# Attention and FFN kernel: high parts of the weights as copies on ScalarE; a small output, values and output weights placed in other steps

## What is computed

```python
def attn(x, W_K, W_Q, W_V, W_O):
    k = jnp.einsum('ihd,bpd->biph', W_K, x)
    q = jnp.einsum('ihd,bpd->biph', W_Q, x)
    v = jnp.einsum('ihd,bpd->biph', W_V, x)
    scores = jnp.einsum('biph,biqh->biqp', k, q)
    mask = jnp.tril(jnp.ones((pos, pos), dtype=x.dtype))
    masked = scores * mask - jnp.float32(10000000000.0) * (1.0 - mask)
    attn = jax.nn.softmax(masked / jnp.sqrt(jnp.float32(d_head)), axis=-1)
    z = jnp.einsum('biqp,biph->biqh', attn, v)
    z_flat = jnp.transpose(z, (0, 2, 1, 3)).reshape(b, pos, -1)
    return jnp.einsum('df,bqf->bqd', W_O, z_flat)

def ffn(x, W1, W2, W3):
    hidden = jax.nn.silu(x @ W1.T) * (x @ W3.T)
    return fwht(hidden) @ W2.T

xn = layernorm(x)
out = x + attn(xn, ...) + ffn(xn, ...)
```

## Time and profile before

| | us |
|---|---|
| three runs | 1448.01, 1448.76, 1451.03; median 1448.76 |
| the profiled execution | 1451.85, its span 1450.0 |
| PE busy | 1351.6 (93%) |
| GpSimd busy | 996.1 (69%) |
| VectorE, ScalarE busy | 957.7 (66%), 931.0 (64%) |

### The profile page before, as it was taken

The page is one execution under the profiler, slowest core; times in us unless marked ns, Lnnn a source line. Parts: engine busy times, 40 slices in busy tenths (PEclk is TensorE's granted clock), DMA queues, the critical chain, the costliest instruction groups (busy, mean ns, idle before and its releaser), DMA issues.

```text
span 1450.0 us, 26628 instructions
## 1 busy us (share of the span) xinstructions
PE 1351.6 (93%) x8104; PEld 1195.5 (82%) x8104; DVE 957.7 (66%) x2133; ACT 931.0 (64%) x1879; POOL 996.1 (69%) x660
## 2 busy tenths in 40 slices
PE   3989999969999999999999999999999999999985
PEld 2778888758888888888888888888888888888875
DVE  7743300277777777777777777777777767777760
ACT  3312244457777777777777777777777777777772
POOL 4420000066979797979797979797979787979785
PEclk8999999989999999999999999999999999999998
DMA  4100056579898989898988898888888888888884
GB/s 147 69 1 0 0 145 186 169 228 286 248 281 259 288 256 286 270 286 253 285 263 280 259 289 268 284 259 280 255 281 270 265 275 266 284 269 288 248 266 153
DMA packets 278459, 335.14 MB, mean 231 GB/s; under 512 B 62736, under 2 KB 251280, under 8 KB 273808
## 3 DMA queue, kind: packets, MB, share of 16 engines
q1 hardware_dynamic: 278416, 334.65, 73.6%
HBM read 173.08 MB, written 161.48 MB: 231 GB/s over the span
## 4 chain that ended last, share of the span: by engine, by line
PE 36%; POOL 23%; issue 20%; DVE 7%; ACT 5%; DMA 4%; SPq 3%; POOLq 0%; DVEq 0%; ACTq 0%
POOL pt_lo L378 15%; PE ps L827 12%; PE ps L828 12%; PE ps L829 12%; POOL acc L369 5%; SPq L276 3%; DMA scratch<-raw 3%; ACT raw L546 2%; DVE had L759 2%; DVE raw L769 2%; POOL v_lo L383 1%; DVE k_lo L672 1%; ACT pt_hi L555 1%; DMA raw<-w3t 1%; DMA pt_lo<-scratch 1%
## 5 line engine op out<-in xcount | busy, mean ns | idle before, releaser
L378 POOL TENSOR_TENSOR pt_lo<-pt_lo,pt_hi 128x640 fp32r<-128x640 f32 (+11 forms) x384 | 661.8, 1753 | 161.2 <-ACT pt_hi L555 161.1
L546 ACT ACTIVATE raw<-ps,had 128x1024 f32<-128x1024 f32 (+7 forms) x384 | 329.5, 867 | 226.0 <-DVE had L762 206.5
L769 DVE STREAM_TRANSPOSE raw<-raw 128x2048 f32<-128x2048 f32 (+15 forms) x256 | 322.0, 1292 | 99.5 <-ACT raw L546 97.2
L827 PE MATMUL ps<-pt_hi,v_hi 128*128 128x256 f32 (+1 forms) x1152 | 326.8, 284 | 29.7 <-POOL pt_lo L378 29.2
L828 PE MATMUL ps<-pt_lo,v_hi 128*128 128x256 f32 (+1 forms) x1152 | 331.7, 288 | 0.0
L829 PE MATMUL ps<-pt_hi,v_lo 128*128 128x256 f32 (+1 forms) x1152 | 329.8, 286 | 0.0
L555 ACT CAST pt_hi<-pt_lo 128x640 fp32r<-128x640 f32 (+11 forms) x384 | 283.4, 819 | 15.1 <-DMA pt_lo<-scratch 14.9
L759 DVE TENSOR_REDUCE had<-ps 128x1 f32<-128x1024 f32 (+1 forms) x256 | 238.0, 950 | 64.7 <-PE ps L829 64.5
L827 PEld LDWEIGHTS ps<-pt_hi,v_hi 128*128 128x128 f32 x1152 | 222.2, 193 | 38.6 <-issue 30.1
L827 PE MATMUL ps<-k_hi,q_hi 128*128 128x512 f32 (+3 forms) x640 | 239.0, 373 | 7.4 <-ACT raw L546 7.4
L829 PE MATMUL ps<-k_hi,q_lo 128*128 128x512 f32 (+3 forms) x640 | 234.6, 366 | 0.0
(11 more groups left out here) (102 smaller groups left out, 2218.3 us busy)
## 6 DMA issues: line engine op xcount, KB each, us to landing
all_values<-raw SPq DMA_DIRECT2D x16, 1024.0 KB, 5.0
v_next<-all_values SPq DMA_DIRECT2D x16, 1024.0 KB, 5.4
scratch<-raw SPq DMA_DIRECT2D x64, 256.0 KB, 5.5
pt_lo<-scratch SPq DMA_DIRECT2D x16, 1024.0 KB, 5.4
scratch<-raw SPq DMA_DIRECT2D x64, 240.0 KB, 5.0
pt_lo<-scratch SPq DMA_DIRECT2D x16, 960.0 KB, 6.0
scratch<-raw SPq DMA_DIRECT2D x64, 224.0 KB, 5.2
pt_lo<-scratch SPq DMA_DIRECT2D x16, 896.0 KB, 4.8
```

The costliest lines, as they stand in the source:

```text
L378: pool.tensor_tensor(lo, lo.bitcast(F32), hi.bitcast(F32), ALU.subtract).then_inc(pt_lo_done, 1)
L546: act.activation(to[:, first // P:(first + n) // P], ps[:, a * BANK:a * BANK + n].rearrange("p (i g k) -> p i g k", g=4, k=BLK), ACT.Exp, ...
L769: dve.transpose(v, v).then_inc(blocked, 1)
L827: pe.matmul(dst, a[0], b[0], start=start, stop=False, skip_group_check=True)
```

## The change

The high parts of the weights are written by ScalarE, as copies, instead of by GpSimd as products with ones: qk_to_hi in step 1 of the head before (and once ahead of the loop), wo_to_hi in step 4. GpSimd keeps the subtractions; that of wq and wk stays in step 2, that of wo moves from step 4 to step 5, in front of line 378. Values block 3 is split in step 0 instead of step 1, on both engines. The add of the small output of step 2 is done in step 3, behind line 378. The guards of the copies (the waits for the loads and for the last product with the old wo) are on ScalarE now; the one for the last projection follows from ScalarE's order.

```diff
--- before.py
+++ after.py
@@ -79,7 +79,7 @@
     KQ_ITEMS = [("Q", 1), ("Q", 2), ("K", 3), ("Q", 3), ("Q", 0), ("K", 0), ("K", 1), ("K", 2)]
 
     V_ITEMS = [3, 2, 0, 1]
-    V_AT = {1: [3], 3: [2], 4: [0, 1]}
+    V_AT = {0: [3], 3: [2], 4: [0, 1]}
     KQ_FIRST = 6
 
 
@@ -199,7 +199,8 @@
         gate_done, hidden_done = sem("gate_done"), sem("hidden_done")
         hid_hi_done, hid_lo_done = sem("hid_hi_done"), sem("hid_lo_done")
         ffn_product, ffn_added = sem("ffn_product"), sem("ffn_added")
-        pool_hi, qk_split, wo_split = sem("pool_hi"), sem("qk_split"), sem("wo_split")
+        wqk_hi_done, wo_hi_done = sem("wqk_hi_done"), sem("wo_hi_done")
+        qk_split, wo_split = sem("qk_split"), sem("wo_split")
         projected, proj_hi, proj_lo = sem("projected"), sem("proj_hi"), sem("proj_lo")
         v_projected, v_copied, v_stored = sem("v_projected"), sem("v_copied"), [sem("v_stored0"), sem("v_stored1")]
         v_moved = sem("v_moved")
@@ -349,19 +350,15 @@
             pool.wait_ge(w2_hi_done, 1)
             pool.tensor_tensor(w2_lo, w2_a, w2_hi.bitcast(F32), ALU.subtract).then_inc(w2_lo_done, 1)
 
-            def split(hi, lo, whole, shape, count, done):
-
-                pool.tensor_tensor(hi, whole, ones[:, :].to_broadcast(shape), ALU.mult).then_inc(pool_hi, 1)
-                pool.wait_ge(pool_hi, count)
-                pool.tensor_tensor(lo, whole, hi.bitcast(F32), ALU.subtract).then_inc(done, 1)
-
-            def split_qk(h, count):
-                pool.wait_ge(qk_loaded, 16 * h + 16)
-                split(wqk_hi[:, :, :], wqk_lo[:, :, :], w_raw[:, 0:2, :], [P, 2, D], count, qk_split)
-
-            def split_o(h, count):
-                pool.wait_ge(wo_loaded, 16 * h + 16)
-                split(wo_hi[:, :], wo_lo[:, :], w_raw[:, 3, :], [P, D], count, wo_split)
+            def split_qk(h):
+                pool.wait_ge(wqk_hi_done, h + 1)
+                pool.tensor_tensor(wqk_lo[:, :, :], w_raw[:, 0:2, :], wqk_hi[:, :, :].bitcast(F32), ALU.subtract
+                                   ).then_inc(qk_split, 1)
+
+            def split_o(h):
+                pool.wait_ge(wo_hi_done, h + 1)
+                pool.tensor_tensor(wo_lo[:, :], w_raw[:, 3, :], wo_hi[:, :].bitcast(F32), ALU.subtract
+                                   ).then_inc(wo_split, 1)
 
             def add(h, z):
                 c = Z_ORDER[z]
@@ -393,20 +390,18 @@
                         if not (first and back) and not (over and not back):
                             add(h + back, z)
                     if s == 2 and more and not over:
-                        pool.wait_ge(projected, kq_count(h, ("Q", 2)))
-                        split_qk(h + 1, 2 * h + 2)
-                    if s == 4 and not over:
-                        if not first:
-                            pool.wait_ge(wo_product, z_count(h - 1, 7))
-                        split_o(h, 2 * h + 3 if more else 2 * h + 2)
+                        split_qk(h + 1)
+                    if s == 5:
+                        split_o(h)
                     for b in [] if over else V_AT.get(s, []):
                         v_to_lo(h, b)
                     hh, ss = step_before(h, s, 2)
                     if not (first and s < 2) and not (over and s >= 2):
                         for n in range(3):
                             p_to_lo(hh, ss, n)
-                    if s in O_SMALL:
-                        back, z = O_SMALL[s]
+
+                    if s != 2 and s in O_SMALL or s == 3:
+                        back, z = O_SMALL[2 if s == 3 else s]
                         if not (first and back) and not (over and not back):
                             add(h + back, z)
 
@@ -417,7 +412,7 @@
                 pool.wait_ge(wv_hi_done, k + 1)
                 pool.tensor_tensor(wv_lo[k][:, :], wv_raw[:, k, :], wv_hi[k][:, :].bitcast(F32), ALU.subtract
                                    ).then_inc(wv_lo_done, 1)
-            split_qk(0, 1)
+            split_qk(0)
             pool.wait_ge(ffn_added, PER_Q * QUARTERS + 1)
             pool.memset(mask[:, :], 0.0).then_inc(mask_ready, 1)
             pool.wait_ge(mask_ready, 1)
@@ -505,6 +500,16 @@
                 act.wait_ge(projected, kq_count(h, item))
                 act.activation(to, ring_bank(item), ACT.Copy, scale=1.0 if which == "K" else SCALE
                                ).then_inc(proj_hi, 1)
+
+            def qk_to_hi(h):
+
+                act.wait_ge(qk_loaded, 16 * h + 16)
+                act.copy(wqk_hi[:, :, :], w_raw[:, 0:2, :]).then_inc(wqk_hi_done, 1)
+
+            def wo_to_hi(h):
+                act.wait_ge(wo_loaded, 16 * h + 16)
+                wait(act, wo_product, z_count(h - 1, 7))
+                act.copy(wo_hi[:, :], w_raw[:, 3, :]).then_inc(wo_hi_done, 1)
 
             def v_copy(i, n):
 
@@ -602,6 +607,10 @@
                         output(h + O_SMALL[s][0], O_SMALL[s][1])
                     if s < 2 and not over:
                         kq_to_hi(h, ("Q", s + 1))
+                    if s == 1 and more and not over:
+                        qk_to_hi(h + 1)
+                    if s == 4 and not over:
+                        wo_to_hi(h)
                     if s == 3 and more and not over:
                         kq_to_hi(h, ("K", 3))
                     if s >= 5 and more and not over:
@@ -615,6 +624,7 @@
                             p_to_hi(hh, ss, n)
 
             act.activation(table_use[:, 2:3], ones[:, :], ACT.Exp)
+            qk_to_hi(0)
             for i in range(TILES):
                 for n in range(QUARTERS):
                     v_copy(i, n)
```

## The result

The changed kernel takes 1502.38 us (median of 6 runs, 1499.65 to 1504.63) against 1448.47 us (6 runs, 1445.97 to 1451.03): 1.037 times the time, 95% interval 1.0354 to 1.0388, 54 us more. The profiled execution has a span of 1502.4 us, against 1450.0.

A forecast was written before the change was run, and what follows sets the result against it. PE was taken to bound the kernel. Lateness of 14 x 2.6 + 3 = 39.4 us plus 20.4 us of clock, 59.8 us on 1448.76, gave 1508.6, told as 1508 us; range 1481 to 1519 us.

The forecast's parts named there:

- What bounds the head: PE, busy 68.26 of 70.60 us in a middle head; relieving GpSimd gives back 1.6% at most, at line 378.
- GpSimd's list: GpSimd's work in program order, from step 3's value subtraction at about 739.97 us to wo_lo's end at 759.06 us.
- The stall: PE waits about 2.9 us for wo_lo at its step 5 output, 2.6 us later in 14 middle heads.
- No slack behind it: After the wait for wo_lo, PE has no wait over 0.2 us, so nothing takes the 2.6 us back.
- The waits ahead of it: PE's waits before wo_lo: the 1.27 us one shrinks to 0.85 us, the 0.28 us one goes without gain.
- The 0.28 us wait: PE's wait at 728.23 us for line 378: goes, but PE then waits longer for z_lo at 737.42.
- The clock: PE's clock falls after every wait for wo_lo: 1.7 us a head, new in 12 heads, 20.4 us.
- The last head: Head 15: PE's output waits 3.3 us for wo_lo, of which the tail keeps about 3 us.
- That the clock stays up: Rival: PE waits for wo_lo but its clock mostly holds, about 1486 us; chance 0.18.
- The high end of the range: Whole kernel: 14 x 2.8 + 14 x 2 + 4 = 71 us more, 1519 us.
- The faster case: Rival: GpSimd's relief reaches PE and wo_lo does not hold it, 0.42 us a head gained, 1443 us; chance 0.05.

The follow-up runs named there:

- run 1: Changed kernel with GpSimd's wo subtraction back in step 4, ahead of the values: 1451.47 us, ratio 1.0003 to the kernel before.
- run 3: Changed kernel with ten useless 512-column matmuls on PE ahead of its wait for wo_lo, in heads 1 to 15: 1485.1 us, ratio 1.0238.
- run 4: Changed kernel with GpSimd's wo subtraction behind the probabilities of step 4, ahead of the small output ending that step: 1465.39 us, ratio 1.0101.
- run 2: Kernel before with only the wo split, both instructions still on GpSimd, moved from step 4 to step 5: 1507.78 us, ratio 1.0386.
- run 6: Changed kernel with the wo subtraction in step 4 behind the values, and ScalarE's wo copy behind its value copies: 1449.18 us, ratio 0.9992.

## Why the prediction was right

The time lay in the range and 6 us under the number, and the path, the wait and the fall of the clock were the ones predicted. Step by step:

- **What bounds the head.** Held. The wait that it called the most that relief could give back, line 378, shrank from 1.27 to 0.87 us (0.85 predicted), and nothing of it was left at the end of the head once the values of step 4 had their say (run 1).
- **GpSimd's list.** From the start of step 3's value subtraction (739.97) to the end of wo_lo (759.06) it gave 19.09 us. Measured: from 833.38 to 852.43, 19.05 us. The price of ScalarE's copy of wo, for which no row stood, is 0.30 us from start to start (841.85 to 842.15), as taken.
- **The stall.** Predicted as 2.6 us a head later, with bounds of 2.2 and 3.1; runs 3 and 4 give 2.66 us and a slope of one. As a wait it shows as 2.45 us, not 2.9. The last matmul ahead of it (849.64) counts as busy for 0.40 us, where the next of its kind starts 0.23 us behind it, so 0.17 us of the stall are hidden. Measured from the mark, PE could have started 0.15 us sooner than before and not 0.3, and it started 21.66 us behind the mark where the prediction has 21.78.
- **No slack behind it.** Held: nothing took the lateness back before the end of the head.
- **The waits ahead of it.** The 0.28 us wait went and gave nothing, as said, though not by a longer wait for z_lo: PE waits 0.48 us for ScalarE's exponentials at the scores of step 3, one place earlier on the same chain.
- **The clock.** The mechanism was right and its size a little off. Taken: 1.7 us in all 14 heads, of which two had it before. Measured: 1.54 us, and in 11 of the 13 head lengths. By the prediction these 13 were to grow by 13 x 2.6 + 11 x 1.7 = 52.5 us; they grew by 969.06 - 921.67 = 47.4. The terms measured give nearly that: 13 x 2.66 + 11 x 1.54 = 51.5, less the 4.3 us by which the two long heads of before stood over 70.57. The prediction put the fall down to three waits of 3.0 to 3.4 us in the trace of before; there is a fourth, of 3.25 us until 77.93, and the lower level followed it too.
- **The last head.** Taken as 3 us. PE starts its output of step 5 at 1447.66 against 1393.91, 53.75 us later, and the span ends 52.4 us later. Of the 53.75 us, 47.1 stood at the last mark and 4.2 are head 14; the other 2.45, by subtraction, are the lateness of this head's own output, which shows as a wait of 3.94 us in place of 0.92 for z_lo. The tail took 1.35 us back; that this is because it hangs on loads and stores is argued. With head 14 (2.6 + 1.7 us) this place was to give 7.3 us; from the last mark to the end of the span it gave 5.3. So 47.4 + 5.3 and -0.3 ahead of the first mark make the 52.4.
- **Rivals and range.** That the clock stays up gave 1486 us, and run 3, which is this rival made true, measured 1485.1, 34.5 us over the kernel before beside it where the rival had 37. Some of this nearness is luck: the rival's sum takes the 0.45 and 1.7 us off once, though two heads had them, and with both off it gives 1484. The advice of the Trainium skill (TensorE: Matmul & The Clock Gate, Why this matters for your kernels) to keep idle gaps between bursts under about 3 us would have let a wait of 2.45 us pass; here the lower level followed it in 11 of 13 heads, so a kernel that keeps to that figure alone may still pay. The high end of the range was worked out with 2.8 us a head and not with the stall's own upper bound of 3.1; with that it would be 4 us higher. The faster case fell as reasoned: GpSimd cannot be early enough, since it waits 0.57 us for ScalarE's copies ahead of the values of step 4.

The stall of head 1 is only 1.36 us, but in its head length stands a wait of 1.72 us for line 375 and the clock fell there too; of the 13 stalls of 2.45 us that follow, 11 were followed by 0.50. It stays open why the other two were not. For the 69 us ahead of these two stalls PE's matmuls stand within 0.1 us where they stand ahead of the stall at 777.73, which was followed by it.

## What to carry to other kernels

Taking work from a busy engine that runs a written order helps only where its next consumer waits for it: here 1.65 us a head taken from GpSimd became waits of GpSimd and gave nothing. Before an instruction is moved in such a list, find the first engine that waits for its result and compare its time with the sum of all that now stands ahead of it; here 8.9 us of GpSimd's list stand between the values of step 4 (842.85) and wo_lo (851.71), and PE was ready some 2.5 us before that was through. And a stall of PE costs more than its length when the clock falls behind it: 2.66 us of lateness cost 4.2.

## What the hardware showed that I had not expected

- In experiment 3 useless matmuls in a stall made the kernel 17 us quicker: with PE at work through the 2.45 us the granted clock stayed at 1.00 from 350 to 1350 us, without them it fell to 0.50 for 3.4 us behind 11 of 13 stalls.
- The length of a wait alone doesn't decide what the clock does. Over the traces of all eleven kernels, PE's waits for GpSimd from 350 to 1376 us: of 47 waits of 1.20 to 1.57 us none was followed by 0.50, of 14 waits of 1.68 to 1.75 us 7 were (both of before, neither of the two of run 6), of 26 waits of 2.45 to 2.54 us (changed, run 2) 22 were.
- Each of those 14 waits stands 5.7 to 5.8 us behind a ScalarE copy of step 3 that had waited for its load. In the kernel before these are the waits of 1.44 us until 456.86 and of 1.29 us until 1164.62, ahead of PE's waits until 462.62 and 1170.39. So its two heads with the clock down began with a late load, not with GpSimd's own work.
